# Expert rows sent back by an indirect scatter and read with plain loads of 120 rows; the zero fill of the experts' input rows moved from the adjacency to the attention heads

## The reference

```
xs = layernorm(x)                                 # 1250 rows of 768
probs = softmax(xs @ Wg)                          # 8 experts
topv, topi = top_k(probs, 2)
for each expert e: rows that chose e go through
    relu(row @ W1[e] + b1[e]) @ W2[e] + b2[e]     # 768 -> 384 -> 768
x = x + sum over k of (topv_k / sum(topv)) * expert_output(k)
xn = layernorm(x)                                 # input of the convolution and the second mixer
```

## Time and profile before

| | |
|---|---|
| median of 3 runs | 2820.5 us |
| the profiled execution | 2820.71 us |
| its span | 2819.0 us |
| TensorE busy | 2686.1 us, 95% |
| VectorE busy | 1481.2 us, 53% |
| ScalarE busy | 889.0 us, 32% |
| POOL busy | 100.9 us, 4% |

### The profile page before, as it was taken

One profiled execution on the slowest core, in us unless ns is written; L12 is line 12 of the kernel. 1 busy time (PEld: TensorE's weight loads), 2 busy tenths in 40 slices (PEclk: granted clock), 3 DMA queues, 4 the chain that ended last, 5 costly groups with the idle time before them and its releaser, 6 DMA issues.

```text
span 2819.0 us, 30928 instructions
## 1 busy us (share of the span) xinstructions
PE 2686.1 (95%) x11845; PEld 1862.8 (66%) x11845; DVE 1481.2 (53%) x2298; ACT 889.0 (32%) x1528; POOL 100.9 (4%) x144
## 2 busy tenths in 40 slices
PE   6999999899989999899959999999999999999999
PEld 5786656698976556577736755566677776555555
DVE  7897899699962555511151210244877774331230
ACT  8895101244421332222221211032644442311210
POOL 1000000000000001100040000000000000000000
PEclk9999999999999999899969999999999999999999
DMA  9904222211030301499946111000200013000000
GB/s 236 334 5 92 96 65 70 72 72 38 19 72 28 73 12 53 139 386 359 358 138 136 39 34 34 0 15 1 90 30 30 30 34 130 6 11 6 11 11 11
DMA packets 131739, 238.12 MB, mean 84 GB/s; under 512 B 18639, under 2 KB 99572, under 8 KB 131118
## 3 DMA queue, kind: packets, MB, share of 16 engines
q1 hardware_dynamic: 116418, 192.97, 22.3%
q0 software_dynamic: 15200, 43.44, 4.6%
HBM read 173.10 MB, written 63.25 MB: 84 GB/s over the span
## 4 chain that ended last, share of the span: by engine, by line
PE 84%; DVE 9%; DMA 3%; ACT 1%; issue 1%; DVEq 1%; POOL 0%; SPq 0%; POOLq 0%; ACTq 0%
PE ps L938 22%; PE ps L1363 15%; PE ps L1320 14%; PE ps L1152 5%; PE ps L955 4%; PE ps L892 4%; PE ps L1062 4%; PE ps L1211 4%; PE ps L1200 4%; PE ps L1264 2%; DVE arena L1990 1%; DVE arena L1983 1%; DVE arena L1798 1%; PE ps L1253 1%; DMA arena<-in_x_dram 1%
## 5 line engine op out<-in xcount | busy, mean ns | idle before, releaser
L938 PE MATMUL ps<-arena 128*125 128x384 f32 x2112 | 697.1, 490 | 6.8 <-DVE arena L1909 2.7
L938 PEld LDWEIGHTS ps<-arena 128*125 128x125 f32 x2112 | 396.1, 189 | 284.3 <-issue 13.8
L1363 PE MATMUL ps<-arena 128*125 128x384 f32 x1280 | 415.4, 488 | 5.8 <-DVE arena L2395 5.8
L1320 PE MATMUL ps<-arena 128*128 128x312 f32 (+1 forms) x1536 | 407.1, 427 | 5.7 <-DVE arena L2395 5.7
L1320 PEld LDWEIGHTS ps<-arena 128*128 128x128 f32 x1536 | 291.6, 190 | 120.0 <-issue 6.6
L1363 PEld LDWEIGHTS ps<-arena 128*125 128x125 f32 x1280 | 241.3, 189 | 179.8 <-issue 8.5
L2395 DVE SCALAR_TENSOR_TENSOR arena<-arena 128x1250 f32<-128x1250 f32 (+3 forms) x175 | 232.0, 1347 | 93.9 <-PE ps L1320 91.6
L1375 ACT ACTIVATE arena<-ps 128x750 f32<-128x750 f32 (+6 forms) x140 | 108.1, 777 | 509.8 <-PE ps L938 201.2
L892 PE MATMUL ps<-arena 128*125 128x380 bf16 x1280 | 213.4, 328 | 11.1 <-DVE arena L1798 11.0
L1909 DVE SCALAR_TENSOR_TENSOR arena<-ps,arena 125x768 f32<-125x768 f32 x30 | 28.7, 955 | 346.9 <-PE ps L1363 292.9
L892 PEld LDWEIGHTS ps<-arena 128*125 128x125 bf16 x1280 | 173.0, 137 | 51.2 <-DVE arena L1798 14.0
(11 more groups left out here) (321 smaller groups left out, 2538.1 us busy)
## 6 DMA issues: line engine op xcount, KB each, us to landing
arena<-in_L_ffn_W_dram SPq DMA_DIRECT2D x54, 1152.0 KB, 7.8
xs_rows<-arena SPq DMA_DIRECT2D x1, 30720.0 KB, 99.5
arena<-in_kw_dram SPq DMA_DIRECT2D x24, 512.0 KB, 4.7
arena<-al_dst POOLq DMA_DIRECT2D x18, 625.0 KB, 4.9
arena<-xs_rows SPq DMA_DIRECT2D x27, 384.0 KB, 7.5
y_rows<-arena POOLq DMA_DIRECT2D x27, 384.0 KB, 6.5
arena<-in_kw_dram SPq DMA_DIRECT2D x6, 1536.0 KB, 10.0
arena<-in_x_dram SPq DMA_DIRECT2D x2, 3600.0 KB
```

Source lines behind the costliest of these rows:

```text
L938: mm = pe.matmul(slot(g)[0:TILE, 512 * half:512 * half + HALF], xt[:, k, i * TILE:i * TILE + TILE], w[:, k, :], start=(k == 0), stop=(k == ...
L1320: mm = pe.matmul(slot(g)[:, 512 * b:512 * b + wd_], w[:, r % 2, ORDER[p], o * P:o * P + P], feat[place(f)][:, lo + b * wd_:lo + b * wd_ + ...
L1363: mm = pe.matmul(slot(g)[0:TILE, 512 * b:512 * b + HALF], fv[:, q, :], w2c[m][q][:, b * HALF:b * HALF + HALF], start=(p == 0 and q == 0), ...
```

## The change

1. **The fill.** `xs_rows` gets rows of 770 numbers (768, the node's number plus one, and the row's own place for the first choice) and 128 rows more. Its fill takes zeros from a piece of `acc` that POOL clears at the third head, in pieces of 154 numbers. SP issues it behind the fifth of a run of five weight loads, during the heads, and waits for it before it reloads x. ScalarE's wait at L1435 goes; POOL waits for the fill before its first scatter.
2. **Dispatch.** The normalised rows lie at a pitch of 770 numbers in reversed order; POOL writes the nodes' numbers with an iota, `slots` copies the place.
3. **The way back.** VectorE works out, for each of an expert tile's 128 rows, where it goes (`destination`): the node's row in the first or second half of `z_rows`, or a spare row. POOL stores each tile with an indirect scatter to `z_rows` instead of a linear store.
4. **The return.** SP, not POOL, loads the rows of each node, now in the order of nodes: first two loads of the last 5 partitions of all ten tiles (`back_rest`), then two loads of 120 partitions for each tile.
5. **The layer norm behind it.** VectorE's bn_stats and bn_aggr go. The second multiply-add accumulates the row's sum, ScalarE squares the centred row with an accumulator, and the root follows. `low_rank(0)` moves behind all ten tiles.

```diff
@@ SP
-            load(xs_d.rearrange("(p q) (c n) -> p (q c) n", p=P, c=3),
-                 zero16.bitcast(F32).unsqueeze(1).broadcast_to([P, 3 * EXP * ROOM // P, 256]), "xs_zero")
             for key in order[0:3]:
                 send(key)
...
             for key in order[5:10]:
                 send(key)
+            sp.wait_ge(ev("zeros"), 1)
+            load(xs_d.rearrange("(p q) (c n) -> p (q c) n", p=P, c=5),
+                 zeros.unsqueeze(1).broadcast_to([P, 5 * (EXP * ROOM + TAU) // P, ROW // 5]), "xs_zero")
             sp.wait_ge(packet_ready, packets["yv", NT - 1] + 1)
+            sp.wait_ge(ev("xs_zero"), 16)
             load(acc[0:120], rows_x[0:120], "x_back")
...
             def dispatched(t):
                 if t >= ERING:
                     sp.wait_ge(packet_ready, packets["sT", t - ERING] + 1)
+                    sp.wait_ge(ev("dest"), t - ERING + 1)
...
+            for q in range(3):
+                sp.wait_ge(ev(f"y_out{q}"), 16 * len(range(q, NTAU, 3)))
+            rows_z = [z_d[1 + k * NODES:1 + k * NODES + NODES].rearrange("(t p) d -> p t d", p=TILE) for k in range(2)]
+            for k in range(2):
+                load(back_all[k][120:TILE], rows_z[k][120:TILE], "back_rest")
+            for t in range(NT):
+                for k in range(2):
+                    load(back[k][t][0:120], rows_z[k][0:120, t, :], f"back{t}")
             sp.wait_ge(ev("ln_x3"), NT)
@@ POOL
             for h in range(HEADS):
+                if h == 2:
+                    emptied(pool, "mP")
+                    pool.memset(zeros, 0.0).then_inc(ev("zeros"), 1)
...
+            pool.wait_ge(ev("A_in"), (HEADS + 1) * NT)
+            own.step(pool.iota(ptab, [[0, 1]], base=0, channel_multiplier=1, ...
+            own.step(pool.iota(spare, [[TAU, NTAU]], base=1 + NODES, channel_multiplier=1, ...
+            own.step(pool.iota(xf_all[:, :, D], [[-TILE, NT]], base=1 + (NT - 1) * TILE, channel_multiplier=1, ...
...
+            pool.wait_ge(ev("xs_zero"), 16)
...
             for n in range(NTAU):
                 emptied(pool, "so", n)
-                pool.dma_start(y_d[n * P:n * P + P], yb[n % 3]).then_inc(ev(f"y_out{n % 3}"), 16)
+                pool.wait_ge(ev("dest"), n + 1)
+                pool.indirect_dma_start(out=z_d, out_offset=bass.IndirectOffsetOnAxis(ap=desti[:, n:n + 1], axis=0),
+                                        in_=yb[n % 3], in_offset=None).then_inc(ev(f"y_out{n % 3}"), 16)
             for q in range(3):
                 pool.wait_ge(ev(f"y_out{q}"), 16 * len(range(q, NTAU, 3)))
-            pool.wait_ge(ev("b1t"), 1)
-            for t in range(NT):
-                for k in range(2):
-                    pool.indirect_dma_start(out=back[k][t], out_offset=None, in_=y_d, ...
@@ ScalarE
-            act.wait_ge(ev("xs_zero"), 16)
...
+            def squares(i):
+                act.wait_ge(ev("centred"), i + 1)
+                act.activation(H[:, i, :], acc[:, i, :], ACT.Square, bias=nmu[:, i:i + 1], accum_out=ssq[:, i:i + 1])\
+                   .then_inc(ev("squared"), 1)
+
             def normalised(i):
-                root_of(i)
...
-            normalised(0)
-            for i in range(NT):
-                if i + 1 < NT:
-                    normalised(i + 1)
-                turned_tile("x3", i, xT)
-                if i == 6:
-                    act.wait_ge(ev("u_ones"), 1)
-                    low_rank(0)
+            own.step(act.activation(primed, onesc, ACT.Sqrt))
+            for i in range(NT):
+                squares(i)
+                root_of(i)
+                if i >= 1:
+                    turned_tile("x3", i - 1, xT)
+                normalised(i)
+            turned_tile("x3", NT - 1, xT)
+            act.wait_ge(ev("u_ones"), 1)
+            low_rank(0)
             low_rank(1)
@@ VectorE
+                chain(dve.tensor_copy(xf[i][:, D + 1:D + 2], slotf[:, 0, i:i + 1]))
...
+            dve.wait_ge(ev("choice_zero"), 1)
+            chain(dve.tensor_scalar(rowp, rowf, ptab[:, 0:1], None, ALU.add))
...
+            def destination(n):
+                dve.wait_ge(ev(f"xs_{n % ERING}"), 16 * (n // ERING + 1))
+                token, first = xs2[n % ERING][:, D:D + 1], xs2[n % ERING][:, D + 1:D + 2]
+                own.step(dve.tensor_scalar(home[:, 0:1], first, rowp[:, n:n + 1], float(NODES), ALU.not_equal, ALU.mult))
+                chain(dve.tensor_scalar(home[:, 1:2], token, 0.0, spare[:, n:n + 1], ALU.is_equal, ALU.mult))
+                chain(dve.scalar_tensor_tensor(out=home[:, 0:1], in0=home[:, 0:1], scalar=home[:, 1:2], in1=token,
+                                               op0=ALU.add, op1=ALU.add))
+                dve.tensor_copy(desti[:, n:n + 1], home[:, 0:1]).then_inc(ev("dest"), 1)
+                dve.wait_ge(ev("dest"), n + 1)
+
             for n in range(NTAU):
+                destination(n)
                 g = take(dve, "so", n)
...
+            dve.wait_ge(ev("back_rest"), 32)
             for t in range(NT):
                 dve.wait_ge(ev(f"back{t}"), 32)
-                for k in range(2):
-                    chain(dve.scalar_tensor_tensor(out=acc[:, t, :], in0=back[k][t], scalar=share[:, k, t:t + 1], ...
-                counted.append(statistics(t, acc))
+                own.step(dve.scalar_tensor_tensor(out=acc[:, t, :], in0=back[0][t], scalar=share[:, 0, t:t + 1], ...
                 if t >= 1:
-                    lowered(t - 1, counted[t - 1])
+                    varied(t - 1)
+                own.settle()
+                chain(dve.scalar_tensor_tensor(out=acc[:, t, :], in0=back[1][t], ..., accum_out=total[:, t:t + 1]))
+                if t >= 1:
+                    lowered(t - 1)
+                dve.tensor_scalar(nmu[:, t:t + 1], total[:, t:t + 1], -1.0 / D, None, ALU.mult).then_inc(ev("centred"), 1)
+                dve.wait_ge(ev("centred"), t + 1)
```

More of the change, by code:

```diff
@@ L58 @@
 ROOM = FULL * TAU
+ROW = 768 + 2
 AHEAD = 6
@@ L340, in build @@
         prod2 = acc_r[:, 2304:3072]
+        zeros = acc_r[:, KT * NODES:KT * NODES + ROW // 5]
         qT = acc_r[:, 0:KT * NODES].rearrange("p (k n) -> p k n", k=KT)
@@ L417, in build @@
         rowi = rcut(NTAU).bitcast(I32)
+        rowp = rcut(NTAU)
+        desti = rcut(NTAU).bitcast(I32)
         cwT = rcut(NODES)
@@ L420, in build @@
         assert ro[0] <= 4700
-        xf = ct_r[0:TILE, 0:NT * D].rearrange("p (t d) -> p t d", t=NT)
+        X0 = R_ACC + R_XT + R_CT - NT * ROW
+        xf_all = arena[0:TILE, X0:X0 + NT * ROW].rearrange("p (t d) -> p t d", t=NT)
+        xf = [xf_all[:, NT - 1 - t, :] for t in range(NT)]
         xfT = [aa_r[:, 750 * n:750 * n + 750].rearrange("p (k n) -> p k n", k=KT) for n in range(2)]
@@ L424, in build @@
         w2s = [r[:, 2304:4608].rearrange("p (k n) -> p k n", k=3) for r in (aa_r[:, 0:4608], aa_r[:, 4608:9216], h_r)]
-        xs2 = [aa_r[:, 9216 + D * n:9984 + D * n] for n in range(ERING)]
+        xs2 = [aa_r[:, 9216 + ROW * n:9216 + ROW * n + ROW] for n in range(ERING)]
         xsT = [ct_r[:, D * n:D * n + D].rearrange("p (k n) -> p k n", k=KT) for n in range(2)]
@@ L428, in build @@
         yb = [ct_r[:, 4608 + D * n:4608 + D * n + D] for n in range(3)]
-        back = [[H[:, t, :] for t in range(NT)],
-                [aa_r[0:TILE, D * t:D * t + D] for t in range(NT)]]
-        xs_d = nc.dram_tensor("xs_rows", (EXP * ROOM, D), F32).ap()
-        y_d = nc.dram_tensor("y_rows", (NTAU * TAU, D), F32).ap()
+        back_all = [H, aa_r[0:TILE, 0:NT * D].rearrange("p (t d) -> p t d", t=NT)]
+        back = [[back_all[k][:, t, :] for t in range(NT)] for k in range(2)]
+        xs_d = nc.dram_tensor("xs_rows", (EXP * ROOM + TAU, ROW), F32).ap()
+        z_d = nc.dram_tensor("z_rows", (1 + 2 * NODES + NTAU * TAU, D), F32).ap()
         nmean = rcut(NT)[0:TILE]
@@ L2323, in _ @@
             give(dve.tensor_copy(WF, slot(g)[0:RANK + 1, 0:HID]), g)
-            counted = []
+            dve.wait_ge(ev("back_rest"), 32)
             for t in range(NT):
                 dve.wait_ge(ev(f"back{t}"), 32)
-                for k in range(2):
-                    chain(dve.scalar_tensor_tensor(out=acc[:, t, :], in0=back[k][t], scalar=share[:, k, t:t + 1],
-                                                   in1=acc[:, t, :], op0=ALU.mult, op1=ALU.add))
-                counted.append(statistics(t, acc))
+                own.step(dve.scalar_tensor_tensor(out=acc[:, t, :], in0=back[0][t], scalar=share[:, 0, t:t + 1],
+                                                  in1=acc[:, t, :], op0=ALU.mult, op1=ALU.add))
                 if t >= 1:
-                    lowered(t - 1, counted[t - 1])
-            lowered(NT - 1, counted[NT - 1])
+                    varied(t - 1)
+                own.settle()
+                chain(dve.scalar_tensor_tensor(out=acc[:, t, :], in0=back[1][t], scalar=share[:, 1, t:t + 1],
+                                               in1=acc[:, t, :], op0=ALU.mult, op1=ALU.add, accum_out=total[:, t:t + 1]))
```

(7 more changed lines are left out.)

55 lines of the change are left out of this document (31 added, 24 removed).

## The result

The changed kernel takes 2840.9 us (median of 4 runs, 2837.77 to 2844.33) against 2818.66 (4 runs): a ratio of 1.0076, 95% interval 1.0065 to 1.0088. It is slower by 0.76%, some 22 us. The prediction said 2823.5 with a range of 2811 to 2834, so it was wrong: too fast by 17 us and outside its range. The profiled execution has a span of 2840.5 us, 21.5 more than the 2819.0 before.

What follows compares the result with a forecast made beforehand. TensorE, busy 95% of the span, was taken as the bound. From the profiled 2820.7: -8.7 + 0 + 0.7 + 0 + 11.1 = 2823.8; against the median 2823.6, stated as 2823.5 us, range 2811 to 2834.

Steps and rivals of the forecast that it cites:

- Part one: Adjacency: with the fill gone, 17 VectorE blocks take 5.21 us each; -8.7 us, bounds 6.8 and 9.5.
- Part two: Heads: the moved fill takes 101 to 168 us in a 196 us gap, not delaying x; cost 0, upper bound 5.
- the fourth: Heads: the fill outlasts them, below 163 GB/s; at 130 GB/s x comes 50 us late, 2870 us; chance 0.04.
- Part three: Dispatch: one chained copy in slots (+0.2) and dearer 3080-byte rows in scatter and load (0.5); together +0.7 us.
- Part four: Experts: VectorE's idle time has room for destination and POOL's indirect issue; cost 0, upper bound 10 us.
- Part five: Return: combine starts 9.4 us later, and the combine through L955's second pass adds 1.7; +11.1 us.
- The start: Return, last store to first combine: 22.4 us against 13.0 before, so 9.4 later; between 11 and 33.5 us.
- The scatter's term: Return: the last rows' indirect scatter takes 6.2 us, between a linear store's 2.59 and 9.18 for two scatters.
- The remainders' 10 us: Return: the two five-partition back_rest loads, 300 KB ahead of tile 0, take 10 us, between 4 and 18.
- the cheap rival: Return: remainders and scatter take 4 us each, the join keeps its length; about 2813 us; chance 0.27.
- Start-up and tile 0's loads: Return: 2 us of load start-up, then 3.9 us for tile 0's two 120-row loads at 190 GB/s.
- The ring: Combine: ScalarE and VectorE wait on each other in a loop of 3.8 us a tile; no gain in pace.

Runs made afterwards that it cites:

- The move alone: Kernel before the change, with only its zero fill sent among the heads in 640-byte pieces and x's reload waiting for it: 2810.9 us, ratio 0.9970.
- a kernel of its own: Changed kernel with its fill put back beside the adjacency in 1024-byte pieces: 2823.2 us, ratio 1.0016 against the old kernel.
- the 128-row kernel: Changed kernel with 640-byte fill pieces, plus z_rows loaded back in runs of 128 rows, 120 and 5 only for the very last tile: 2803.4 us, ratio 0.9947.

## Why the prediction was wrong, by its steps

- **Part one, the adjacency: right, and a little small.** What was forecast of the profile, no issue in front of L1806 and blocks of 5.21 us, came: 17 blocks take 88.8 us (L1840 from 35.51 to 124.35) instead of 97.3, which is 8.5 of the 8.7. The products start 10.0 us earlier, just past the bound of 9.5, because the first block too comes 1.6 us earlier (35.51 against 37.08). How much of that is the fill's is open: the first block lies between 35.4 and 36.7 in the kernels whose fill is moved, and between 36.3 and 37.1 in the three that have it in front. The move alone gave 9.0 us.
- **Part two, the fill among the heads: this step failed.** The fill was put at 101 us by bytes and 168 by pieces, in a gap of 196, so that x would not be delayed. It took 221.7, above both bounds. Both came from the old fill, whose 1024-byte pieces all began at multiples of 1024; neither looked at where the new ones begin. The runs put this in its place: pieces whose ends are off a 32-byte grain in memory cost half as much again to twice as much (fills of 204.5 to 277.7 us against 131.8), and the 616-byte fill takes as long beside the adjacency (225.9 us) as among the heads. With 640-byte pieces on the grain the kernel is 28.2 us faster, and there the two bounds do hold: 131.8 us lie between 101 by bytes and 162 by pieces. The rival that came true is the fourth, given 4 in 100; its threshold held (144 GB/s against its 163), and so, nearly, did its price of one us per us late. That `al_dst` rows land in 7.5 us instead of 4.9 and hold up nobody was right (one wait of 2.9 us, 2.8 before), and so was the rest of the step.
- **Part three, dispatch: right** (0.7, measured 0.4).
- **Part four, experts: right** (0, measured 0.3).
- **Part five, the return: right in sign, too big** (+11.1; +3.4 in the ledger, +4.2 as a kernel of its own). The start was put at 22.4 us and took 17.6.
  - The scatter's term failed: I took 6.2 between a linear store and a queue of two scatters, and alone it lands in 3.00.
  - From the scatter's landing to the combine I had 16.2 us, and it took 14.6. The remainders' 10 us were near (10.4 with the better load, some 9.6 without), and the cheap rival, 4 us, was not. That was luck in part: no row gave the 10, a choice between 4 and 18 that was said to be nearer the row without a companion and is nearer the other. Start-up and tile 0's loads were 5.9 in the sum; the 128-row kernel takes 4.2 for them.
  - The ring has 3.49 us a tile, not 3.8, and the 120-row loads need 3.1 (236 GB/s), not 3.9; from the combine's start to the second pass there are 46.1 us instead of 47.3, so that term was -1.2, not +1.7. What was wrong in it is the six tiles at +0.25: the recorded pace of 3.8 less the old 3.73 doesn't give that number, and they gave -1.4; the other two parts came (tile 0's L1615 1.7 us sooner, forecast 1.9; 8.4 us between the passes, forecast 8.7).
  - The prediction's own sign, an idle time of VectorE under 15 us, came if the last wait is taken (14.37) and not with the 2.86 before the small copy (17.2); the second pass stands 65.3 us behind the last copy, where 73 were forecast.
  - The rule of the Trainium skill that was weighed there (DMA: Bandwidth & Descriptors, "Why a DMA increments its semaphore by 16 and not by 1": five engines for five rows, an estimate of 4.9 us) gave half or less of what the remainders cost, so a share of the engines alone isn't their price. For 125 rows it gives five engines too, and there the trace agrees: a mean share of 0.32 of the 16 engines, 126 GB/s, and a combine that waits 3.6 us a tile, where loads of 128 rows leave no wait behind the second tile. For the remainders themselves no window shows it, as other loads run beside them.
- **The sum.** Against the profiled execution the prediction had 2823.8. Part one takes 1.3 off, part two adds 28.6 (0.3, 26.5 and 1.8 of the ledger), parts three and four come to the 0.7 they were given, and the return takes 8.7 off (11.1 against 3.4 - 0.8 - 0.2). That makes 2842.4; the profiled execution took 2842.2.

The change's own three parts are worth -9 to -10 (the move, if the fill fits), +28 (the fill's pieces) and +4 (the return), and with pieces on the grain and 128-row loads they are worth -15.

## What to carry to other kernels

When a layout gains a few columns, look at what it does to the address of every piece that is written: a row of 3080 bytes instead of 3072 is 0.3% more bytes, and a fill cut along such rows took 222 us instead of 132. A fill need not follow the rows; cut the flat memory into pieces on the grain. A long transfer is hidden only if everything behind it on its queue is hidden too; taking away the wait doesn't help what stands behind it in order. And remainders of five rows can stand in front of everything (some 10 us here): reading three rows too many into 128 partitions was cheaper.

## What the runs showed of the hardware

- Writes to memory in pieces of 640 bytes ran at 299 GB/s with both ends at multiples of 32 bytes and at 154 with both off it (starts of 8 modulo 32). The source's address in the arena, 8 bytes further on, made no difference (300). The Trainium skill (DMA: Bandwidth & Descriptors, "How a descriptor splits into AXI transactions") tells of a start off a multiple of 256 bytes that makes a transfer read more than it needs; it says so of reads. Here half of the unshifted pieces begin off 256 and all of those shifted by 32 bytes do, and both fills ran at 298 to 299 GB/s, so for these writes that grain isn't the one that counts.
- The busy share of the engines doesn't tell this: it is 1.01 to 1.11 for the fast fills and 1.15 to 1.17 for the slow ones. The GB/s beside it do.
- VectorE's register loads are slowed by the 1024-byte fill at 340 GB/s (share 0.98), and not by the 616-byte fill at 155 GB/s (share 1.18). What slows them is thus not how busy the engines are; what it is stays open.
- Loads of 125 rows kept the 16 engines of DMA at a mean share of 0.32 and moved 126 GB/s; loads of 120 rows moved 236 and loads of 128 rows 336, both at a share near 1. The difference between the last two is unexplained.
- An indirect scatter of 128 rows of 3072 bytes, alone, landed in 3.00 us, the linear store in 2.59.
